# A fused graph network on one core: the radial network, the sort by source and the edge attributes move out of the opening stage

## What is computed

```python
x = ln(x + L0(x))   # 2 rounds of attention over edges (8 heads) + feed-forward
x = ln(x + L1(x))   # attention summed by src (4 heads)
x = ln(x + L2(x))   # two hypergraph convolutions: 4 products with the count matrix
x = ln(x + L3(x))   # messages weighted by the attributes and the radial network

# L3, per edge
h = silu(edge_attr_10 @ fc_w1 / sqrt(10)) * 1.679177
msg_rad = h @ fc_w2 / sqrt(64)                  # one number per edge
messages = angular(x[src], edge_attr_4) * msg_rad
agg = segment_sum(messages, dst) / sqrt(16)
```

## Time and profile before

| | us |
|---|---|
| Median of 3 runs (lowest, highest) | 6446.02 (6445.78, 6452.75) |
| Profiled execution | 6405.28 |
| Its span, first to last instruction | 6404.1 |
| Busy: TensorE / VectorE / GpSimd / ScalarE | 4183.3 / 3234.6 / 3052.6 / 1186.7 |

### The profile page before, as it was taken

The page is one execution under the profiler, slowest core; times in us unless marked ns, Lnnn a source line. Parts: engine busy times, 40 slices in busy tenths (PEclk is TensorE's granted clock), DMA queues, the critical chain, the costliest instruction groups (busy, mean ns, idle before and its releaser), DMA issues.

```text
span 6404.1 us, 64980 instructions
## 1 busy us (share of the span) xinstructions
PE 4183.3 (65%) x18847; PEld 3189.9 (50%) x18847; DVE 3234.6 (51%) x6404; ACT 1186.7 (19%) x3608; POOL 3052.6 (48%) x2628
## 2 busy tenths in 40 slices
PE   1875444345587444435559655667999999977775
PEld 0553222233355322223336534446888888866665
DVE  1856554588824555568881356664000100157767
ACT  0111111100022111110012111113320100044443
POOL 0044666788884466678888366650000000036664
PEclk9997666689999666659989578788999999968888
DMA  7135777656522677756642111114975455435554
GB/s 293 38 75 148 246 248 245 187 106 136 105 6 38 206 251 242 248 126 137 137 91 1 22 24 25 24 22 130 243 203 152 123 152 152 134 122 170 162 162 130
DMA packets 617769, 874.38 MB, mean 137 GB/s; under 512 B 212943, under 2 KB 422398, under 8 KB 617298
## 3 DMA queue, kind: packets, MB, share of 16 engines
q0 software_dynamic: 235984, 384.87, 25.3%
q1 hardware_dynamic: 291468, 435.37, 22.6%
q10 hardware_dynamic: 89974, 49.94, 2.5%
HBM read 644.32 MB, written 225.60 MB: 136 GB/s over the span
## 4 chain that ended last, share of the span: by engine, by line
PE 44%; DVE 25%; issue 13%; another core or an unknown queue 7%; SPq 5%; DVEq 3%; ACT 2%; DMA 1%; POOL 0%; ACTq 0%; POOLq 0%
PE bank L2059 17%; DVE arena L1130 7%; DVE arena L1221 4%; PE bank L2129 3%; PE bank L1979 3%; PE bank L1815 3%; DVE arena L1114 3%; DVE arena L1181 3%; PE bank L1989 3%; PE bank L2130 2%; PE bank L1929 2%; DVE arena L1401 2%; SPq L540 2%; PE bank L1927 1%
## 5 line engine op out<-in xcount | busy, mean ns | idle before, releaser
L730 POOL DMA_INDIRECT arena<-YT,arena x416 | 415.7, 999 | 1632.0 <-DMA YT<-arena 1384.2
L730 POOL DMA_INDIRECT arena<-KVT,arena x832 | 814.5, 979 | 674.9 <-DVE arena L1184 255.3
L2059 PE MATMUL bank<-arena 128*128 128x256 f32 x5000 | 1102.9, 380 | 7.8 <-DMA arena<-AM 6.2
L2059 PEld LDWEIGHTS bank<-arena 128*128 128x128 f32 x5000 | 941.5, 190 | 132.3 <-issue 6.4
L1130 DVE TENSOR_TENSOR arena<-arena,bank 128x273 f32 (+2 forms) x1664 | 716.9, 431 | 363.6 <-DVE arena L1130 172.2
L766 POOL DMA_INDIRECT ATT<-arena x391 | 666.9, 1706 | 122.9 <-issue 116.6
L752 POOL DMA_INDIRECT sc<-arena x391 | 664.3, 1699 | 123.2 <-issue 115.8
L1907 PE MATMUL bank<-arena 128*128 128x273 f32 x1664 | 442.7, 409 | 399.3 <-DVE arena L1221 395.7
L1181 DVE TENSOR_TENSOR arena<-arena,bank 128x256 f32<-128x256 f32 x832 | 300.7, 415 | 655.9 <-remote 445.7
L1907 PEld LDWEIGHTS bank<-arena 128*128 128x128 f32 x1664 | 302.5, 191 | 539.3 <-DVE arena L1221 442.7
L730 POOL DMA_INDIRECT arena<-X1T,arena x416 | 399.2, 960 | 336.6 <-issue 121.9
(11 more groups left out here) (297 smaller groups left out, 6478.4 us busy)
## 6 DMA issues: line engine op xcount, KB each, us to landing
VE<-arena SPq DMA_DIRECT2D x208, 512.0 KB
arena<-VE SPq DMA_DIRECT2D x208, 512.0 KB, 3.5
arena<-ATT SPq DMA_DIRECT2D x250, 320.0 KB, 3.2
arena<-AM SPq DMA_DIRECT2D x250, 320.0 KB, 2.9
ATT<-arena POOLq DMA_DIRECT2D x5, 8000.0 KB, 72.8
AM<-arena ACTq DMA_DIRECT2D x125, 192.0 KB, 3.6
AM<-arena ACTq DMA_DIRECT2D x125, 128.0 KB, 3.1
arena<-KVT,arena POOLq DMA_INDIRECT x832
```

Source lines behind the costliest of these rows:

```text
L730: GP.indirect_dma_start(out=ring[:, i % n, k, :], out_offset=None, in_=table, in_offset=bass.IndirectOffsetOnAxis(ap=idx[:, 4 * i + k:4 * ...
L2059: mm = P.matmul(bank[j][:, 0:256], left[:, 128 * j:128 * (j + 1)], right[:, u, :], start=(u == 0), stop=(u == W - 1))
```

## The change

1. The radial network, in 98 steps of 256 columns, goes into the value loop `v1`; banks 6 and 7 are its own, and the loop's sums rotate through six banks in place of eight. The attributes are loaded and scaled after that loop and written to a new DRAM table `ATTR`.
2. `SW` carries each edge's row number in `ATTR` and zeros for the attributes. It is written as soon as the edges are in. After the gathers of layer L1, GpSimd adds the attributes into `PA[:, :, 2:6]` with 416 indirect transfers; VectorE and ScalarE wait for them before layer L3.
3. The sort by source goes into the `s_in` loop (counting) and into `k0` (one VectorE operation per step).
4. The edge list comes as one array in one transfer; the window starts are found with narrow operations and small matrix products.
5. `ATT` is cleared in 25 pieces of 1.6 MB, one in flight at a time: five before the fetch and 20 after it. The wait for it moves from the projections to the edge flags, since the zeros now lie in `B`. The tables `sb` are no longer cleared.
6. The fetch keeps its split between SyncE and GpSimd (`fetch_mine` is unchanged).

```diff
@@ SyncE
+        SY.dma_start(keys.rearrange("p k c -> p (k c)"), a["edges"]).then_inc(keys_in.sem, 16)
+        SY.dma_start(XE, a["x"][0:768, :].rearrange("(w p) f -> p w f", p=128)).then_inc(xe_in.sem, 16)
...
+        SY.wait_ge(*edges_made("rows", 1))
+        SY.dma_start(flat(SW[0:R1], C), PW.rearrange("p c k -> p (c k)")).then_inc(sw_out.sem, 16)
...
         SY.wait_ge(*sw_out(2))
+        SY.wait_ge(*edges_made("starts", 1))
@@ SyncE, before and in the reads of the value loop
+            if l == 1:
+
+                SY.wait_ge(*fc_clear("v1", 2))
+                SY.dma_start(fc1[0:10, 0:64], a["L3_gnn_fc_w1"]).then_inc(fc_in.sem, 16)
...
             for i in range(G):
+                if l == 1 and i < 2:
+                    load_emb(i)
+                elif l == 1 and i >= 15 and i % 6 == 3:
+                    load_emb(i // 6)
@@ SyncE, after the value loop
                     SY.wait_ge(*added(f"v{l}", T))
+                    if l == 1:
+                        SY.dma_start(at4.rearrange("p c k -> p (c k)"), a["attr"]).then_inc(attr_in.sem, 16)
@@ GpSimd
+        def clear(pieces):
+            for k in pieces:
+                if k:
+                    GP.wait_ge(*table_clear(k))
+                part = every[0:NODES].rearrange("(p c) -> p c", p=128)[:, 3200 * k:3200 * (k + 1)]
+                GP.dma_start(part.rearrange("p (a b) -> p a b", b=1600),
+                             zero.unsqueeze(1).to_broadcast([128, 2, 1600])).then_inc(table_clear.sem, 16)
+        clear(range(5))
+
+        GP.wait_ge(*sw_out(2))
+        GP.wait_ge(*edges_made("starts", 1))
...
+                        GP.dma_start(PA[:, 4 * i + j, :], SW[bass.ds(first, 128), :]).then_inc(fetched[2 + i % 2].sem, 16)
+        GP.end_ifs()
+        clear(range(5, PIECES))
@@ GpSimd, after the gathers of layer L1
+        GP.wait_ge(*attr_out(1))
+        for c in range(T):
+            GP.indirect_dma_start(
+                out=PA[:, c, 2:6], out_offset=None, in_=ATTR,
+                in_offset=bass.IndirectOffsetOnAxis(ap=PA[:, c, 0:1].bitcast(I), axis=0), bounds_check=R1 - 1,
+                compute_op=ALU.add).then_inc(attr_back.sem, 16)
@@ VectorE, window starts
+        for b in range(25):
+            ins = V.scalar_tensor_tensor(t1, PW[:, :, 1], float(128 * (b + 1)), ones[:, 0:1].to_broadcast([128, C]), ALU.is_lt,
+                                         ALU.mult, accum_out=lastF[:, b:b + 1])
...
+        ask(V.tensor_tensor(dshift[:, 1:24], dshift[:, 1:24], lastF[:, 0:23], ALU.subtract))
+        after_starts(True)
@@ VectorE, s_in loop
         for w in range(W):
+            d.settle()
+            d.mark(V.scalar_tensor_tensor(t1, kw, float(w), ones[:, 0:1].to_broadcast([128, C]), ALU.is_equal,
+                                          ALU.mult, accum_out=cnt[:, w:w + 1]))
@@ VectorE, load_and_project
-            V.wait_ge(*zeros_out(12))
-            V.wait_ge(*table_clear(6))
-            V.wait_ge(*sw_out(2))
@@ VectorE, before the edge flags
         V.wait_ge(*small_out("prep", asked[0]))
+        V.wait_ge(*zeros_out(4))
+        V.wait_ge(*table_clear(PIECES + 1))
+        V.wait_ge(*sw_out(2))
@@ VectorE, key loop
+                if l == 0:
+                    source_place(i)
@@ VectorE, source_place
+            elif i % 4 == 0:
+                d.mark(V.tensor_scalar(of_bucket, kw, float(b), None, ALU.is_equal))
+            elif i % 4 == 1:
+                d.mark(V.tensor_tensor_scan(rank, of_bucket, of_bucket, 0.0, ALU.add, ALU.max))
+            elif i % 4 == 2:
+                d.mark(V.scalar_tensor_tensor(rank, rank, offw[:, b:b + 1], of_bucket, ALU.add, ALU.mult))
+            else:
+                d.mark(V.tensor_tensor(posw, posw, rank, ALU.add))
@@ VectorE, after v1
+                V.wait_ge(*radial_mm("v1", HIDDEN))
+                d.then(V.tensor_scalar(rr, bank[7][:, 0:C], cst, None, ALU.mult))
+                V.wait_ge(*attr_in(1))
+                V.tensor_tensor(at4, at4, rr.unsqueeze(2).to_broadcast([128, C, 4]), ALU.mult).then_inc(attr_made.sem, 1)
@@ ScalarE, v1
+                if l == 1 and i < HIDDEN:
+                    S.wait_ge(*hidden_mm("v1", i + 1))
+                    if i >= 3:
+                        S.wait_ge(*radial_mm("v1", i - 2))
+                    S.activation(hid[:, i % 3, :], bank[6][:, 256 * (i % 2):256 * (i % 2) + 256], ACT.Silu,
+                                 scale=float(np.float32(1) / np.float32(np.sqrt(10.0)))).then_inc(hidden.sem, 1)
@@ TensorE, v1
+        def radial(i):
+
+            if i < HIDDEN:
+                if i >= 2:
+                    P.wait_ge(*hidden("v1", i - 1))
+                P.wait_ge(*emb_in[(i // 6) % 2](i // 12 + 1))
+                P.matmul(bank[6][:, 256 * (i % 2):256 * (i % 2) + 256], fc1[0:20, :],
+                         emb[(i // 6) % 2][0:20, (i % 6) * 256:(i % 6) * 256 + 256],
+                         start=True, stop=True).then_inc(hidden_mm.sem, 1)
+            if 1 <= i <= HIDDEN:
+                P.wait_ge(*hidden("v1", i))
+                for k in range(2):
+                    c_ = 4 * (i - 1) + 2 * k
+                    mm = P.matmul(bank[7][:, c_:c_ + 2], hid[:, (i - 1) % 3, k * 128:k * 128 + 128], fc2, start=True, stop=True)
+                mm.then_inc(radial_mm.sem, 1)
...
+                if l == 1:
+                    radial(i)
```

More of the change, by code:

```diff
@@ L858, in buckets @@
                 add_up(nb, dense_base)
-            ins = V.tensor_tensor(off[:, 0:nb], base[:, 0:nb], bank[3][:, 0:nb], ALU.add)
-            if used is not None:
-                ins.then_inc(used.sem, 1)
-                V.wait_ge(*used("gen", asked[0]))
-            else:
-                d.then(ins)
+            V.tensor_tensor(off[:, 0:nb], base[:, 0:nb], bank[3][:, 0:nb], ALU.add).then_inc(gen_used.sem, 1)
+            V.wait_ge(*gen_used("gen", asked[0]))
             d.then(V.tensor_tensor(off[:, 1:nb], off[:, 1:nb], lastF[:, 0:nb - 1], ALU.subtract))
@@ L1529, in scalar_engine @@
     def scalar_engine():
-        for i in range(49):
-            S.wait_ge(*hidden_mm("prep", i + 1))
-            if i >= 2:
-                S.wait_ge(*radial_mm("prep", i - 1))
-            S.activation(hid[i % 2], bank[i % 2][:, :], ACT.Silu,
-                         scale=float(np.float32(1) / np.float32(np.sqrt(10.0)))).then_inc(hidden.sem, 1)
         def copy_turned(name, w, cols):
@@ L1739, in scalar_engine, with v_banks @@
             roots("out", part, stats_out)
+    def v_banks(l, i):
+        return [(4 * i + k) % (6 if l else 8) for k in range(4)]
     def x1_copy(w):
@@ L1903, in add_up @@
             for k in range(4):
-                if i >= 2:
-                    P.wait_ge(*added(name, 4 * (i - 2) + k + 1))
+                before = 4 * i + k - (6 if name == "v1" else 8)
+                if before >= 0:
+                    P.wait_ge(*added(name, before + 1))
                 r = rhs(k)
@@ L2154 @@
         x = np.ascontiguousarray(val)
+        if name == "dst":
+            continue
+        if name == "src":
+            dst = np.ascontiguousarray(inputs["dst"])
+            name = "edges"
+            x = np.concatenate([by_partition(x, NP), by_partition(dst, NP), by_partition(dst[1:], NP),
+                                by_partition(dst[APART:], 2 * NP)], 1)
         if name == "edge_attr_10":
```

365 lines of the change are left out of this document (174 added, 191 removed).

## The result

The changed kernel takes 6232.95 us (median of 4 runs, 6229.89 to 6235.22), the kernel before 6449.39 beside it (6445.78 to 6457.43): the ratio is 0.9662, 95% interval 0.9646 to 0.9679, or 216.4 us less. The forecast was 6263 us.

What follows compares the result with a forecast made beforehand. No engine binds throughout; the opening lies ahead of everything. Terms -233 + 18 + 14 + 8 + 10 = -183 took the profiled 6405.3 to 6222, or 6263 us against the 6446.0 median; own range 6215 to 6315, 8-in-10 range 6195 to 6345.

Steps and rivals of the forecast that it cites:

- Edges, checks, window starts: First steps of the new opening: edges in at 8 us, row words to 15, window starts to 38, small sums to 50.
- Clearing: GpSimd's 20 pieces after its fetch, each waiting for the one before: 6.8 us a piece, 136 us, to 322.
- Cover: In the opening, VectorE's own path ends at 268 us, hidden by 57 us behind the clearing, which ends about 325.
- rival (a): Opening: clearing pieces under 4.1 us, so VectorE's own path binds at 268 us; total 6209 us; 9 in 100.
- The flags: Edge flags at the opening's end start at 325 us in place of 558.4: -233 us, bounds -287 and -199.
- Source order, 18: One more VectorE operation per step of `k0`, mostly hidden in waits for gathers: +18 us, bounds 0 and 63.
- Radial, 14: In `v1`, radial steps of 1.90 us make TensorE the bound by 0.14 us: 98 steps, +14, bounds 0 and 35.
- Attributes, 8: After the last window of `v1`, VectorE waits 6.2 us for the attributes' load, then scales 1.79: +8 us.
- Gathers sharing hop 0, 10: Attribute gathers hidden on GpSimd but sharing DMA with hop 0: +10 us, from nothing to 46.
- (b): Rival: the loops pay in full, 63, 35, 8 and 46 us given back against -233; total 6365 us; 19 in 100.
- (c): Rival: TensorE's clock falls to 0.66 in `v1`, +216 us in place of 14; total 6465 us; 3 in 100.
- (d): Rival: attribute gathers not hidden, holding up layer L3 from 3.33 us each; 6750 us at 4.5 each; 3 in 100.

Runs made afterwards that it cites:

- first pair: The changed kernel beside the kernel before, first measurement: 6232.95 us against 6449.39, ratio 0.9662.
- group 2: Four kernels on one chip: changed kernel again (6236.12 us), clearing spaced (6174.23), no radial network (6238), pieces without waits (6235); kernel before beside them 6453 us.
- group 1: Four kernels on another chip: kernel before again (5929 us), changed kernel with clearing later (5761), without attribute gathers (5709), with two more scans in `k0` (5742).
- group 3: Four kernels on a third chip: before without radial network (6358 us), before with edges first (6364), before with both (6283), changed with source order in the cover (6195).
- two cures: Kernel before without the radial network, or with clearing writes behind the edges' load: flags at 517.0 and 526.6 us, with both 421.9, against 558.4.

## Why the prediction was right, and where its terms were off

The time, 6233, lies in the forecast's own range of 6215 to 6315, and the mechanism is the one forecast: flags and first gathers behind the last clearing piece, every loop nearly as it was. One of the signs named for it did not come: the step of `v1` stayed at 3.87 us with TensorE still waiting. And one sign of being wrong did come, the fetch slowed by the clearing. Neither weighed on the time.

- *Edges, checks, window starts.* 8, 15, 38 and 50 were forecast; the rows show 7.74, 14.9, 37 and 46.5. A count took 0.85 us and its accumulated output 0.08, not 0.3.
- *Fetch.* GpSimd's took 134.6 us (135). SyncE's took 196 us (179): it ran to 244 beside the clearing, and took 178 us where the clearing was elsewhere (47.3 to 225.4, the run with the clearing out of the opening). VectorE waited 14.25 us for it, hidden by the longer wait.
- *Clearing,* the term of 6.8 us a piece: it measured 6.33, and 6.0 alone, so the chain ended at 310 and not at 322. The figure taken from the nearest row, 5.7 us of transfer, was good (5.9); the issue was overpriced.
- *Cover.* VectorE's own path was forecast at 268, against 325. Without the clearing the flags started at 252: the cover was 59 us, and rival (a)'s gain of that size was there, as the run with spaced clearing took it.
- *The flags,* -233: measured -247. The 27.5 us behind them were taken as fixed; they became 35.8, with waits in TensorE's 26 small turns. They took 35 to 36 us in three profiles (first pair, group 2) in which the gathers start with the flags, 23 to 24 in group 1 where they do so too, and 22.9 to 29.1 elsewhere. The cause wasn't isolated. To the first product the gain is 238.8.
- *Source order, 18:* 0 where `k0` takes 660 us, 9 to 11 where it takes 531. The bounds of 0 and 63 held; the value was too high for the pair forecast.
- *Radial, 14:* 4.6 in the pair of profiles. The term that was mis-sized is "half of 2.00 + 1.80": it gave 1.90 us for TensorE's radial step, which measured 1.30 (below). TensorE never became the bound.
- *Attributes, 8:* 6.7 us between the last weighting and the bias addition (15.0 against 8.3); the wait was 3.82 us and not 6.2.
- *Gathers sharing hop 0, 10:* none. The bound of 46 took 0.49 us of DMA time for each; 178 of them raised the share by 0.11 in 345 us, 0.21 us each, to 1.01 and not to 1.15.

These terms give -239 + 0 + 5 + 7 + 0 = -227, and the pairs measure -216 and -217. The 10 us between are less than the spread of single gather-fed loops within one group (646.8 to 655.7 in L1, for identical code) and aren't placed. The forecast's -183 was 33 us short: 37 in the three small terms and 6 in the opening, less these 10.

*The radial step.* A step of 256 columns was taken as half a step of 512 in the chain. That chain, in the stretch around the two lines that the forecast read, held no idle time of TensorE (its window, and the two groups in order of time):

```profile
200.00:210.00 10.00, 10.00 (x30) 6.83 (x30) 9.96 (x2) 1.79 (x3) 0.00 (x0) 1.00 0.04 12
...
198.06 2.07 PE L1774 MATMUL bank<-arena 20*128 20x512 f32 x2
200.06 1.87 PE L1781 MATMUL bank<-arena 128*128 128x2 f32 x8
```

Two products of 512 columns took 2.07 us there, two of 256 took 0.69 in `v1`; eight small ones took 1.87, four 0.61. Half the work took a third of the time, at a granted clock of 1.00 there and 0.99 from 2780 us on in `v1`. Why isn't shown. With 2.11 + 1.30 = 3.41 us of products in a step, TensorE stayed under VectorE's 3.87.

*The profiled execution.* The text put the 40.7 us between it and the median on top without asking what they were. They are the surroundings of that execution: its L1 loop and last loop, 652.6 and 666.2, are those of group 3, where the kernel before took 6401; the changed kernel's were those of group 2. Had the two traces been taken as a pair, 42 us would have been charged to a loop that the change doesn't touch. Without these 40.7 us the forecast would have read 6222, nearer to 6233, but only by luck, since its gain was 33 us short.

*The rivals.* (a) didn't occur: the pieces took 6.3 us and not 4.1. (b) keeps only the attributes' 8. (c), the falling clock, shows in traces: 0.84 for 22 us of `v1`, and in the run without attribute gathers 0.60 for 21 us and 0.73 for 25, where four steps took 5.5 to 6.2 us in place of 3.87, 7.8 of the 11 us; it recovered each time. (d) had 583 us in hand.

*The two rules of the Trainium skill.* On the page "SBUF — State Buffer", section "SBUF: two separate sides", the traces show a gather's issue stopped by wide operations, and little of it by narrow ones. The wide case, GpSimd's row and VectorE's:

```profile
312.13 4.91 POOL L736 DMA_INDIRECT arena<-KVT,arena  x1 [0.30 <-issue]
315.03 1.89 DVE L1110 TENSOR_SCALAR arena<-arena 128x3328 f32<-128x3328 f32 x1
```

This issue took 4.91 us in place of 0.95. It began while the flags' first operation ran (311.30, 3.62 us) and ended 0.12 us after L1110; the kernel before had the same at 559.50, 4.68 us, ended 0.12 us after its L1097. By that rule, the traces agree here. For the narrow operations in `k0` they side with the lower figure: not 59 us, but 0 to 11; the scans added on purpose paid 0.21 us each of 0.83.

On the page "DMA: Bandwidth & Descriptors", section "Issuing engines are not separate DMA queues", the row is the 110.56 us that reads issued by SyncE waited behind writes issued by ScalarE, with the DMA share at 1.00: by that rule, the trace agrees. But it does not make sharing a cost in itself, since hop 0 carried 178 gathers with add beside its own reads, at share 1.01, without taking longer.

## What to carry to other kernels

When several things hold an opening, removing one hands its wait to the next: two cures gave 41 and 32 us alone and 137 together, so cost such a change as a whole, from the new chain. A bulk write that nobody needs soon belongs where an engine is computing and DMA is little used (a share of 0.22 to 0.33 there), one piece in flight at a time: the same 41 MB cost some 60 us on GpSimd's queue in the opening, 114 all at once in front of an aggregation, and nothing spaced under a feed-forward stage. Before comparing two traces, check that loops which the change doesn't touch took the same time in both.

## What the runs showed that was not expected

- The same kernel took 5925, 6401 and 6453 us in three groups, on three chips. Only loops fed by indirect gathers differ (over all profiles: `k0` 531 to 666, L1 533 to 671, the last loop 570 to 708 us); hops (1259 to 1264) don't, nor the opening of the kernel before (586 and 580).
- Zeros read from DRAM, 25,600 floats repeated 16 times, serve to clear as zeros in on-chip memory do, but not faster. Issued at once, 25 such pieces moved at 324 GB/s, about 5 us each; the pieces from on-chip memory, issued without waits, at 407 to 416 GB/s with the fetch beside them. One at a time they lay (1638.8 - 1467.1) / 24 = 7.15 us apart, against 6.0 to 6.3, though in another stage.
- A fetch of 260 small transfers (4 KB, 1.8 us each in the median) took 178 us without bulk writes, 196 beside large writes of which one was in flight at a time, and 235 beside those issued without gaps.
